# Counting of edges beside the experts: one wide comparison a group for the near one-hots

## What is computed

```
h = x @ W
norm = dinv[src] * dinv[dst]
msg = h[src] * norm[:, None]
return jax.ops.segment_sum(msg, dst, num_segments=n) + b
```

```
for e in range(E):
    h = jax.nn.gelu(xf @ W1[e] + b1[e], approximate=False)
    out = out + w_dense[:, e:e + 1] * (h @ W2[e] + b2[e])
```

## Time and profile before

| | us |
|---|---|
| median of 3 runs | 6315.04 (6313.85 to 6325.95) |
| profiled execution, its own time | 6313.73 |
| its span | 6312.1 |
| near one-hots of layer 0, first to last start | 1687.3 to 1922.7 |
| near one-hots of layer 1, first to last start | 3479.6 to 4122.1 |
| VectorE busy in the whole span | 4142.4 (66%) |
| TensorE busy in the whole span | 4962.2 (79%) |

### The profile page before, as it was taken

The page is one execution under the profiler, slowest core; times in us unless marked ns, Lnnn a source line. Parts: engine busy times, 40 slices in busy tenths (PEclk is TensorE's granted clock), DMA queues, the critical chain, the costliest instruction groups (busy, mean ns, idle before and its releaser), DMA issues. The chain is left out here.

```text
span 6312.1 us, 118827 instructions
## 1 busy us (share of the span) xinstructions
PE 4962.2 (79%) x25970; PEld 3714.9 (59%) x26035; DVE 4142.4 (66%) x13016; ACT 2792.1 (44%) x8212; POOL 3057.2 (48%) x3493
## 2 busy tenths in 40 slices
PE   5720999996377868888883899969999997888685
PEld 4510777775254556666662666645657775666575
DVE  7771666664587779999996777753433336888612
ACT  0010777774115246666663111124533333888423
POOL 4786777776474068888870222213220001777321
PEclk9975999997696789999995999989989998999698
DMA  6521444454487222222232565543420002666454
GB/s 241 182 66 49 124 125 125 126 119 102 129 252 184 58 67 68 70 69 67 68 60 77 165 187 182 176 137 114 144 80 10 10 10 65 159 161 160 81 175 118
DMA packets 787124, 719.98 MB, mean 114 GB/s; under 512 B 349384, under 2 KB 692973, under 8 KB 786382
## 3 DMA queue, kind: packets, MB, share of 16 engines
q1 hardware_dynamic: 596344, 372.06, 20.9%
q0 software_dynamic: 120064, 280.26, 16.8%
q10 hardware_dynamic: 70486, 65.22, 3.0%
HBM read 520.74 MB, written 201.60 MB: 114 GB/s over the span
## 5 line engine op out<-in xcount | busy, mean ns | idle before, releaser
L1122 POOL DMA_INDIRECT l3e_rows<-table,l3e_idx x440 | 435.2, 989 | 733.3 <-DVE l3e_idx L1144 604.7
L1122 POOL DMA_INDIRECT l0e_rows<-table,l0e_idx x440 | 426.6, 969 | 154.3 <-issue 128.3
L1122 POOL DMA_INDIRECT l1e_rows<-table,l1e_idx x440 | 429.7, 977 | 121.4 <-issue 121.4
L3491 ACT ACTIVATE l1e_weighted<-l1e_rows,l1e_power 128x64 f32<-128x64 f32 x1760 | 463.0, 334 | 14.7 <-ACT l1e_power L3482 7.3
L890 POOL DMA_INDIRECT records_by_src<-l0n_rec_src,l0n_pos_at_src x390 | 395.6, 1014 | 115.4 <-issue 108.8
L1431 PE MATMUL l0e_ps_w<-l0e_wf,l0e_hidT 128*128 128x256 f32 x1760 | 436.3, 381 | 0.0
L3432 PE MATMUL l1e_ps_row<-net_ident,l1e_logit 128*128 128x128 f32 x1760 | 276.8, 280 | 127.3 <-DVE l1e_logit L3627 126.4
L2798 ACT ACTIVATE l1fg_hT<-l1fg_ps_h,l1fg_b_cols 128x256 f32<-128x256 f32 x256 | 107.3, 470 | 530.5 <-PE l1fg_ps_h L2741 530.5
L1431 PEld LDWEIGHTS l0e_ps_w<-l0e_wf,l0e_hidT 128*128 128x128 f32 x1760 | 301.0, 191 | 63.3 <-issue 0.3
L2165 ACT ACTIVATE l2fe_hT<-l2fe_ps_h,l2fe_own,l2fe_own 128x320 f32<-128x320 f32 x320 | 197.5, 617 | 310.8 <-PE l2fe_ps_h L2115 310.6
L3446 PE MATMUL l3e_ps_s<-l3e_weighted,l3e_onehot 128*128 128x257 f32 x880 | 246.7, 425 | 94.3 <-ACT l3e_weighted L3493 94.1
(11 more groups left out here) (850 smaller groups left out, 14965.7 us busy)
## 6 DMA issues: line engine op xcount, KB each, us to landing
counts<-l1f_total ACTq DMA_DIRECT2D x272, 128.0 KB, 4.3
l1fg_w_in<-in_L_ffn_W SPq DMA_DIRECT2D x32, 1024.0 KB
l1fg_w_out<-in_L_ffn_W SPq DMA_DIRECT2D x32, 1024.0 KB
records_by_dst<-l0n_blank_dst SPq DMA_DIRECT2D x5, 6512.0 KB
l3e_rec<-records_by_dst SPq DMA_DIRECT2D x110, 296.0 KB, 3.4
l2d_counts<-counts SPq DMA_DIRECT2D x208, 128.0 KB, 2.4
l2d_counts<-counts POOLq DMA_DIRECT2D x192, 128.0 KB, 2.7
l3fg_w_in<-in_L_ffn_w SPq DMA_DIRECT2D x16, 1024.0 KB, 7.3
```

The lines of the kernel that those rows point to most:

```text
L1122: pool.indirect_dma_start(at(self.rows[b], k, self.width), None, self.table, bass.IndirectOffsetOnAxis(self.idx[b][:, k:k + 1], 0)).then_i ...
L3491: act.activation(out[:, h, 0:each], g.rows[b][:, lo:lo + each], ACT.Copy, scale=power[b][:, m * heads + h:m * heads + h + 1])
```

## The change

The near one-hots of all items of a group are made by one `tensor_tensor` comparison, `mark_near`, ahead of the group's marks: the row of numbers is read again for each half of each item, and each of the group's scalars is read 128 times in a row. `mark` keeps only the far one-hots. `hot_near` becomes two buffers by the group's parity, of 768 columns in layer 0 and 2304 in layer 1, and `near_now` is bfloat16, so that row, scalars and result all are. TensorE waits on a further semaphore, `near_marked`, ahead of the first count of a group. Item counts, buffers of the far one-hots, matmuls, adds and transfers are as they were.

```diff
--- before.py
+++ after.py
@@ -2380,13 +2380,14 @@
         self.each = self.items.EACH[layer]
         self.first = groups * sum(self.items.EACH[:layer])
         assert groups == self.items.GROUPS and self.each % self.HOTS == 0
-        self.hot_near = [s.sb(f"hot_near{b}", [P, 2 * P], BF16) for b in range(self.HOTS)]
+        self.hot_near = [s.sb(f"hot_near{b}", [P, 2 * self.each * P], BF16) for b in range(2)]
         self.hot_far = [s.sb(f"hot_far{b}", [P, 2 * SPAN], BF16) for b in range(self.HOTS)]
         self.total = [s.sb(f"total{b}", [P, SPAN], U16) for b in range(2 * self.each - 1)] + [self.items.carry]
-        self.near_now = [s.sb(f"near_now{b}", [P, 2 * self.each]) for b in range(2)]
+        self.near_now = [s.sb(f"near_now{b}", [P, 2 * self.each], BF16) for b in range(2)]
         self.far_now = [s.sb(f"far_now{b}", [P, 2 * self.each]) for b in range(2)]
         self.keep_now = [s.sb(f"keep_now{b}", [P, self.each]) for b in range(2)]
         self.scalars_taken = s.sem("scalars_taken")
+        self.near_marked = s.sem("near_marked")
         self.marked = s.sem("marked")
         self.item_summed = s.sem("item_summed")
         self.total_ready = s.sem("total_ready")
@@ -2414,21 +2415,29 @@
         dve.tensor_copy(self.keep_now[b][:, :], self.of_group(self.items.keep, g, 1)).then_inc(self.scalars_taken, 1)
         dve.wait_ge(self.scalars_taken, 3 * g + 3)
 
+    def mark_near(self, dve, g, b):
+
+        wide = [P, 2 * self.each, P]
+        dve.wait_ge(self.item_summed, g * self.each + 1)
+        dve.tensor_tensor(tiled(self.hot_near[b][:, :], P), self.items.row_near[:, :].unsqueeze(1).to_broadcast(wide),
+                          self.near_now[b][:, :].unsqueeze(2).to_broadcast(wide), ALU.is_equal).then_inc(self.near_marked, 1)
+
     def mark(self, dve, g, b, u):
         dve.wait_ge(self.item_summed, g * self.each + u + 1)
         for m in range(2):
-            dve.tensor_scalar(at(self.hot_near[u % self.HOTS], m, P), self.items.row_near[:, :], at(self.near_now[b], u * 2 + m, 1),
-                              None, ALU.is_equal)
             ins = dve.tensor_scalar(at(self.hot_far[u % self.HOTS], m, SPAN), self.items.row_far[:, :], at(self.far_now[b], u * 2 + m, 1),
                                     None, ALU.is_equal)
         ins.then_inc(self.marked, 1)
 
     def count(self, pe, ps, g, b, u):
         n = g * self.each + u
+        if u == 0:
+            pe.wait_ge(self.near_marked, g + 1)
         pe.wait_ge(self.marked, n + 1)
         pe.wait_ge(self.total_ready, n + 1)
         for m in range(2):
-            ins = pe.matmul(ps[:, (b * self.each + u) % 2, :], at(self.hot_near[u % self.HOTS], m, P), at(self.hot_far[u % self.HOTS], m, SPAN), start=m == 0, stop=m == 1)
+            ins = pe.matmul(ps[:, (b * self.each + u) % 2, :], at(self.hot_near[b], u * 2 + m, P),
+                            at(self.hot_far[u % self.HOTS], m, SPAN), start=m == 0, stop=m == 1)
         ins.then_inc(self.item_summed, 1)
 
     def add(self, dve, ps, g, i, b, u):
@@ -2858,6 +2867,7 @@
             def count_first(g, i, b):
                 if counting:
                     counting.take_scalars(dve, g, b)
+                    counting.mark_near(dve, g, b)
                     for u in range(2):
                         counting.mark(dve, g, b, u)
                     count(g, i, b, 0, min(FC, counting.each))
```

## The result

The changed kernel takes 6394.9 us (median of 4 runs, 6390.43 to 6395.51), the kernel before, on the same chip, 6318.2 us (median of 4). The ratio is 1.0121, 95% interval 1.0106 to 1.0136: slower, by 77 us. The prediction said 6389 us. The profiled execution has a span of 6393.7 us and its own time is 6395.32, against 6312.1 and 6313.73 of before.

The account below looks back on a forecast made before the run. Layer 1 was taken as bound by VectorE's order (head latency, then its pace), layer 0 by GpSimd's transfers and index copies; 68.8 - 35.2 + 36 + 4 = +74 us on 6313.7, plus 1.3 to the median, gave 6389 us, range 6341 to 6413.

Parts of the forecast that it names:

- Length of the comparison: Layer 1's wide comparison of 2304 columns: 2.48 us, scaled from rows of 1600 and 640 columns with the same access pattern.
- the double rate: Rival: two columns pass per cycle, the comparison takes 1.28 us, about 6310 us in all; chance 0.09.
- Head, +2.15 a group: Layer 1, before a group's first count: the wide comparison replaces two short ones, +2.15 us a group, +68.8 us in all.
- Recovered, -1.10: Layer 1, behind the head: TensorE no longer waits for VectorE, -1.10 us a group, -35.2 us in all.
- the small gaps that were foreseen: Sign expected in the changed trace: VectorE has small gaps between add and mark.
- Falls, +36: Layer 1: longer TensorE waits lower its clock in two groups of three, 21 x 1.7 = +36 us.
- the 2.54 us wait: A TensorE idle wait elsewhere in the earlier trace with no clock fall behind it, cited for the rival without falls.
- the case without falls: Rival: layer 1's waits of 3.1 to 3.5 us leave TensorE's clock up, 6353 us; chance 0.20.
- Layer 0, +4: Layer 0's groups: the head grows by 0.54 us, partly hidden by late rows; +4 us, bounds 0 and 17.
- its first case: The forecast case itself, with clock falls in two of three layer 1 groups: 6389 us, chance 0.62.
- VectorE's total with the head covered, 6295: Rival: TensorE's other work covers the head's latency, so VectorE's saved time counts, -20 us, 6295; chance 0.04.
- GpSimd held up, 6417: Rival: GpSimd stands still during the wide comparison, layer 0 pays up to 0.87 us a group, +28 us; chance 0.05.

Follow-up runs that it names:

- the kernel with step 1: The changed kernel with layer 1's one-hots laid out item last, so that all operands of the comparison have step 1; 6325.2 us, ratio 1.0011.
- kernel with filled time: The changed kernel with the matmuls of one block of hide ahead of layer 1's first count issued three times instead of once; 6357.2 us, ratio 1.0062.
- layer 0 alone: The changed kernel with layer 1's short near comparisons put back, so the wide comparison is in layer 0 only; 6324.1 us, ratio 1.0008.

## Why the prediction was right

**Length of the comparison.** 2.48 us was taken from the 1600 and 640 column rows, over the 1.28 of the double rate (2.44 + 0.06 is 2.50, not 2.48, a slip worth 0.6 us in all); the trace shows 2558 ns against 2.55 foreseen, and 2.48 from start to start (3846.81 to 3849.29). The double rate exists, as the kernel with step 1 shows, and the change doesn't meet its condition: the rival was a real one, and the choice by the access pattern of the nearest rows decided it.

**Head, +2.15 a group.** Measured +2.14. TensorE's wait is 3.27 us each where 3.4 was said, 98.2 us and the 4.4 beside it; the 1.26 us that 3.4 was built on were 0.1 too many by the missing records.

**Recovered, -1.10.** The first count to the transposes is 9.50 us as forecast, 1.02 and 1.09 less than in the two groups of the earlier trace rows; head and recovery together are 21.60 - 20.51 = +1.09 us a turn (means of the two lengths), against 1.05. The kernel with filled time gives 32.6 us for 31 turns, where 68.8 - 35.2 = 33.6 for 32 groups stood. VectorE's new waits for counts, 82 of them, are the small gaps that were foreseen.

**Falls, +36.** 20 in 31 turns against 21 in 32 groups; 1.69 us each against 1.7; 34.5 us when they are taken away alone. The size was right, but "two groups in three" was a guess between bounds of 0 and 54 us, so that it fits to 2 us is luck. What picks the groups was not found: of the waits of 3.1 us 9 in 16 were followed by a fall, of the 3.5 us ones 11 in 14. The prediction gave the 2.54 us wait as one without a fall; the same line of the same stage has two more of that length that it leaves out, and the clock fell at both (0.57 granted in the windows around and behind them):

```profile
5292.89 0.69 PE L336 MATMUL l3n_turn<-net_ident,l3n_xn 128*128 128x128 f32 x2 [2.56 <-DVE l3n_xn L318]
5302.65 0.69 PE L336 MATMUL l3n_turn<-net_ident,l3n_xn 128*128 128x128 f32 x2 [2.57 <-DVE l3n_xn L318]
```

```profile
5292.00:5296.00 4.00, 3.11 (x10) 2.62 (x11) 3.34 (x18) 0.93 (x3) 0.00 (x0) 0.57 0.00 0
5302.00:5306.00 4.00, 3.35 (x10) 2.79 (x11) 3.34 (x16) 1.06 (x3) 0.00 (x0) 0.57 0.00 0
```

So what spoke for the case without falls was weaker than it looked, and length alone doesn't tell which wait costs a fall. (What the prediction cites from the Trainium skill, "TensorE: Matmul & The Clock Gate", stands there in the section "Why this matters for your kernels".)

**Layer 0, +4.** The trace shows +4.8, but a kernel without the wide comparison there shows as much. The term is not refuted, and not shown; it is small, and nothing hangs on it.

**The rivals.** No falls, 6353: the kernel with filled time is that rival made real, at 6357. (The forecast says that from about seven falls on the sum is nearer to its first case; the middle between 6353 and 6389 lies at 18 / 1.7, some 11 falls.) The double rate, 6310: made real by the layout, 6325, a loss of 7 us with layer 0's share and two falls in it. VectorE's total with the head covered, 6295: covered by moving the comparison it is 6253, since the 1.26 us that were there before go as well. GpSimd held up, 6417: the mechanism is real and was given 0.05; the row that spoke against it showed transfers beside short instructions, none as long as the new comparison. In layer 1 the hold costs nothing (below), since nobody waits for it. In layer 0 single transfers are held too, but the means stay near those of the earlier trace rows: 985 ns against 988 for the gathers and 1041 against 1034 for the scatters, under 1 us in all. With layer 0 alone they are 1019 and 1048, some 3 us in all; whether layer 0's few us are this hold is not shown. Of the 6 us between 6389 and 6395, 3 are the kernel before, at 6318.2 beside the changed one and 6315.0 when the forecast was made; the other 3 are within what single executions differ by.

## What to carry to other kernels

Fusing many small instructions into one makes their sum shorter and their first result later. Before doing it, look for who waits for the first result: if that engine stands still, pay the whole length less what stood there before, and count the clock as well, which here doubled the loss. The same fused instruction, issued one group earlier behind buffers that the change already had, turned +77 us into -66 (52 of these came with the short comparisons in that place too); look for the stretch in which the issuing engine waits, and put it there. When the price of an operation with two 2-byte inputs hangs on its rate, look at whether an operand stands still along the innermost index, not only at its type.

## What the runs showed of the hardware

**A transfer of GpSimd is held while VectorE compares.** In the head shown above, the indirect transfer that starts at 3847.37 lasts 2.90 us and ends 0.90 us behind the 2.56 us comparison; the next, at 3850.57, takes 1.00. So the held one ends as if it had begun when the comparison was over. Groups of instructions of 3480 to 4200:

```profile
L2923 POOL DMA_INDIRECT outputs<-l1fg_y,l1fg_target x60 | 122.5, 2041 | 461.6 <-DVE l1fg_y L2859 452.5 <-issue 9.1
```

The mean was 1101 ns before, is 2041 with a comparison of 2558, 1446 with one of 1358, and 1012 where the comparison was moved away from the transfer. The mean is over the two transfers of a group, of which the first is held; it follows the comparison's length. It cost nothing here because GpSimd idles 452.5 us in front of these transfers. The 0.96 us comparison of layer 0 does the same to a transfer that starts inside it, which ends 0.84 us behind the comparison:

```profile
1690.44 0.96 DVE L2422 TENSOR_TENSOR l0f_hot_near<-l0f_count_row_near,l0f_near_now 128x768 bf16<-128x768 bf16 x1
1690.74 1.50 POOL L890 DMA_INDIRECT records_by_dst<-l0fg_rec_dst,l0fg_pos_at_dst  x1 [0.31 <-issue]
```

"SBUF — State Buffer" of the Trainium skill, section on who interferes with whom, says that a VectorE instruction with two inputs in SBUF contends with a GpSimd instruction that reads SBUF; the trace agrees, if an indirect transfer counts as such an instruction. The same section reports a probe in which `tensor_tensor` did not stall a DMA; for indirect transfers issued by GpSimd the runs here show the contrary.

**Idle time in front of busy time can be cheaper filled than left.** 256 matmuls whose results were already there made the kernel 38 us faster, since waits of 1.4 to 2.0 us had no fall behind them in 31 turns, and waits of 3.1 to 3.5 had 20. With waits of 2.2 us on average and 2.7 at most (the kernel at step 1) there were two, behind the two longest. These are counts for this loop; no length was found from which on a fall is sure.
